# Four places of weight matrices in rotation: expert 0's first matrix loaded in the projection, the first half of the tokens routed earlier

## The reference

```
x = x + attn(layernorm(x)) @ Wr + br          # 2048 tokens, D = 1024, 16 heads of 64; mask multiplies the scores
f = layernorm(x)
p = softmax(f @ router_w + router_b)          # 8 experts, the best two of a token, weighted with their p
shared = gelu(f @ sw1 + sb1) @ sw2 + sb2      # hidden 2048
mixed  = sum over the two chosen experts of p_e * (gelu(f @ rw1[e] + rb1[e]) @ rw2[e] + rb2[e])
x = x + shared + mixed
```

## Time and profile before

| | us |
|---|---|
| median of 3 runs | 1258.63 (1258.38 to 1302.35) |
| the profiled execution | 1259.96 |
| its span, slowest core (core 2) | 1258.4 |
| spans of the 8 cores | 1252.9 to 1258.4 |
| PE busy | 1134.6 (90%) |
| ACT, DVE, POOL busy | 505.7, 446.3, 225.1 |
| HBM read, written | 241.40 MB, 74.45 MB |

### The profile page before, as it was taken

How to read it: one execution, slowest core, us unless ns; L and a number is a source line. 1 busy time by engine, 2 the same in 40 slices (tenths; PEclk the granted TensorE clock), 3 DMA queues, 4 the chain that set the end, 5 groups by cost and what they waited for, 6 DMA issues and landing times.

```text
span 1258.4 us, 20967 instructions; the slowest of 8 cores (1252.9 to 1258.4 us)
## 1 busy us (share of the span) xinstructions
PE 1134.6 (90%) x7570; PEld 595.2 (47%) x7648; DVE 446.3 (35%) x617; ACT 505.7 (40%) x671; POOL 225.1 (18%) x389
## 2 busy tenths in 40 slices
PE   5988888888889989519999999999999999999998
PEld 3533333333334434217475757565666666444443
DVE  6456667767657740000101010101111010134476
ACT  5768888888862233213131322222222221122100
POOL 1022222222210017501111111111111110212230
PEclk9999999999999979859999999999999999999999
DMA  6769557673756529999999999996969995485484
GB/s 191 258 182 226 135 135 117 175 162 106 115 118 231 199 80 238 241 203 188 189 200 252 244 200 192 192 272 111 255 128 199 190 192 114 149 288 194 150 302 167
DMA packets 66212, 235.34 MB, mean 187 GB/s; under 512 B 8256, under 2 KB 9152, under 8 KB 64576
## 3 DMA queue, kind: packets, MB, share of 16 engines
q0 software_dynamic: 34592, 123.87, 51.3%
q1 hardware_dynamic: 31520, 110.10, 25.8%
HBM read 241.40 MB, written 74.45 MB: 251 GB/s over the span
## 4 chain that ended last, share of the span: by engine, by line
PE 76%; DVE 7%; issue 7%; DMA 4%; ACT 4%; POOL 2%; DVEq 0%; another core or an unknown queue 0%; SPq 0%; ACTq 0%; POOLq 0%
PE PM L810 20%; PE PM L825 17%; PE PM L774 9%; PE PM L754 6%; PE SLOT L646 4%; PE PM L714 4%; PE NUM L664 4%; PE DEN L671 3%; ACT PT L1184 3%; DVE RC L931 3%; PE PM L832 2%; DMA XTILE<-xe 2%; POOL xe L517 2%; DMA xe<-XN,IDX 2%; DVE DS L922 2%
## 5 line engine op out<-in xcount | busy, mean ns | idle before, releaser
L1184 ACT ACTIVATE PT<-SLOT 128x1024 bf16<-128x1024 f32 (+1 forms) x320 | 262.6, 903 | 44.5 <-PE SLOT L646 43.7
L1108 DVE TENSOR_TENSOR YST<-PM,B2BC 128x512 f32<-128x512 f32 x64 | 44.2, 691 | 476.2 <-PE PM L825 442.5
L1240 ACT ACTIVATE HE_T<-PM,B1ALL 128x576 bf16<-128x576 f32 x128 | 94.9, 741 | 254.0 <-PE PM L810 254.0
L664 PE MATMUL NUM<-PT,VX 128*64 128x512 bf16 (+3 forms) x640 | 115.4, 360 | 18.6 <-DVE NS L919 15.1
L810 PE MATMUL PM<-XET,WB 128*128 128x288 bf16 x1024 | 127.8, 288 | 1.4 <-ACT XET L1223 1.1
L810 PE MATMUL PM<-XET,WA 128*128 128x288 bf16 x1024 | 126.1, 286 | 0.0
L646 PE MATMUL SLOT<-QT,KT 64*128 64x512 bf16 (+3 forms) x640 | 100.6, 354 | 17.7 <-ACT PT L1184 13.8
L671 PE MATMUL DEN<-PT,ONES 128*64 128x512 bf16 (+3 forms) x640 | 110.4, 349 | 5.9 <-DVE DS L922 5.9
L810 PEld LDWEIGHTS PM<-XET,WB 128*128 128x128 bf16 x1024 | 100.5, 98 | 28.8 <-issue 3.0
L825 PE MATMUL PM<-WB,HE_T 128*128 128x512 bf16 x496 | 113.0, 379 | 0.8
L825 PE MATMUL PM<-WA,HE_T 128*128 128x512 bf16 x497 | 112.2, 379 | 0.8
(11 more groups left out here) (124 smaller groups left out, 1129.1 us busy)
## 6 DMA issues: line engine op xcount, KB each, us to landing
WA<-w2cat POOLq DMA_DIRECT2D x48, 512.0 KB, 13.8
WA<-w1cat POOLq DMA_DIRECT2D x40, 512.0 KB, 24.1
WB<-w1cat POOLq DMA_DIRECT2D x40, 512.0 KB
XT<-xtok SPq DMA_DIRECT2D x32, 512.0 KB, 3.8
wbf<-WA SPq DMA_DIRECT2D x8, 2048.0 KB, 6.8
yd<-YST SPq DMA_DIRECT2D x32, 512.0 KB, 9.6
WB<-w2cat POOLq DMA_DIRECT2D x24, 512.0 KB, 23.3
xe<-ZERO SPq DMA_DIRECT2D x16, 512.0 KB, 5.1
```

What stands on the lines that cost most here:

```text
L664: e.matmul(NUM[64 * hh:64 * hh + 64, lo:512], VX[:, kc * D + c * 128 + 64 * hh:kc * D + c * 128 + 64 * hh + 64], pt(n)[:, hh * 512 + lo:(h ...
L1184: e.activation(heads(pt(n), lo, 512), heads(slot(r), lo, 512), AF.Exp, scale=0.125).then_inc(expd, 1)
L1240: e.activation(HE_T[:, ht * CAP:(ht + 1) * CAP].rearrange("p (h q) -> p h q", h=2), heads(PM1[:, (n % 2) * 1024:(n % 2 + 1) * 1024], 0, CA ...
```

## The change

Expert 0's first matrix goes to `WA2` (was V's place) and its second to `WB1`; even experts use `WA2` and `WB1`, odd ones `WA1` and `WB2`. The hidden halves that are spilled, and the x1 rows at the end, move to `WB2`; so ACT waits for the stores of x1 before it writes the second half. POOL issues the 8 pieces of expert 0's first matrix in the projection, one behind each of the first 8 tiles, and no longer between the scatters. The scatters of half 0 start at projection tile 14. `choose(0)` comes one tile sooner on DVE and `place(0)` two, `positions(0)` follows them on PE. Three small constants are loaded from ACT's queue instead of SP's.

```diff
--- before.py
+++ after.py
...
@@ -273,7 +274,7 @@
                 ZERO = sb(s1, "ZERO", [128, 2 * D], BF16)
             SB2BC = sb(s, "SB2BC", [128, D], F32)
 
-        G12, X1D = WA1.ap().bitcast(F32), WA2.ap().bitcast(F32)
+        G12, X1D = WA1.ap().bitcast(F32), WB2.ap().bitcast(F32)
 
         with ExitStack() as p:
             XTR = ps(p, "XTR", [128, 4 * 1024], BF16)
@@ -308,14 +309,14 @@
             return XLN2T[:, at:at + n]
 
         def w_first(x):
-            return WA1 if x % 2 else WB1
+            return WA1 if x % 2 else WA2
 
         def w_second(x):
-            return WA2 if x % 2 else WB2
+            return WB2 if x % 2 else WB1
 
         def hidden(k):
 
-            return (XLN2T[:, 0:8192], WA2[:, 8192:16384], H1D[:, 0:8192], H1D[:, 8192:16384])[k]
+            return (XLN2T[:, 0:8192], WB2[:, 8192:16384], H1D[:, 0:8192], H1D[:, 8192:16384])[k]
 
         def wbf_rows(x, i):
             return wbf[x * 256 + i * 128:x * 256 + (i + 1) * 128, :]
@@ -334,10 +335,6 @@
 
         def run_sync(e):
             for t in range(NMT):
-                if t == 1:
-                    e.dma_start(out=EPS[:], in_=c_eps).then_inc(eps_in, 16)
-                    e.dma_start(out=IDB[:], in_=c_idb).then_inc(idb_in, 16)
-                    e.dma_start(out=ONES[:], in_=c_ones).then_inc(ones_in, 16)
                 if t >= 4:
                     e.wait_ge(xb_done, t - 3)
                 e.dma_start(out=ring(XT, t % 4), in_=xtok[t * 128:(t + 1) * 128, :]).then_inc(xt_in[t % 4], 16)
@@ -468,7 +465,7 @@
 
         def spill(e, k):
             e.dma_start(out=h1d[k * 128:(k + 1) * 128, :],
-                        in_=WA2[:, k * 8192:(k + 1) * 8192]).then_inc(h1_out, 16)
+                        in_=WB2[:, k * 8192:(k + 1) * 8192]).then_inc(h1_out, 16)
 
 
         def run_gpsimd(e):
@@ -510,30 +507,34 @@
                         e.dma_start(out=BRR[:], in_=br_row).then_inc(brr_in, 16)
                         e.dma_start(out=RWW[:], in_=rww_rl).then_inc(rww_in, 16)
 
-            e.wait_ge(zero_out, 16 * 3 * NE)
+            e.wait_ge(av_mm, len(SCORES))
+            for i in range(PIECES):
+                e.wait_ge(op_mm, i + 1)
+                piece(WA2, w1cat[1], i, w1_in[0])
 
 
             def scatter(k, t):
                 e.indirect_dma_start(xe, bass.IndirectOffsetOnAxis(IDX[:, k * NMT + t:k * NMT + t + 1], 0),
                                      xn2(t), None).then_inc(scat, 16)
 
+            e.wait_ge(zero_out, 16 * 3 * NE)
             e.wait_ge(rt, RT_IDX)
-            e.wait_ge(op_mm, NMT)
             for t in range(HALF):
                 for k in range(2):
-                    e.wait_ge(s_mm1, 2 * t + k + 1)
+                    n = 2 * t + k
+                    if n < 6:
+                        e.wait_ge(op_mm, 14 + n // 2)
+                    else:
+                        e.wait_ge(s_mm1, n - 5)
                     scatter(k, t)
-                piece(WB1, w1cat[1], t, w1_in[0])
             e.wait_ge(rt, RT_HALF + RT_IDX)
             for t in range(HALF, NMT):
-                e.wait_ge(s_mm1, HALF + t + 1)
+                e.wait_ge(s_mm1, t + 3)
                 for k in range(2):
                     scatter(k, t)
 
-            e.wait_ge(xn2_done, NMT)
-            for j in range(4):
-                e.wait_ge(x1_out[j], 16 * 4)
-            load(WB2, w2cat[1], w2_in[0])
+            e.wait_ge(op_mm, NMT)
+            load(WB1, w2cat[1], w2_in[0])
 
 
             for x in range(1, NEXP):
@@ -700,8 +701,6 @@
                 m.then_inc(pos_mm, 1)
 
             for i in range(NMT + 3):
-                if i == HALF + 6:
-                    positions(0)
                 if i < NMT:
                     t = i
                     if t >= 2:
@@ -715,6 +714,8 @@
                                      WRF[:, kc * D + h * 512:kc * D + (h + 1) * 512], start=(kc == 0), stop=False)
                         m = e.matmul(psv, ONES[0:1, 0:128], BRR[0:1, h * 512:(h + 1) * 512], start=False, stop=True)
                     m.then_inc(op_mm, 1)
+                if i == HALF + 4:
+                    positions(0)
                 if 2 <= i < NMT + 2:
                     t = i - 2
                     e.wait_ge(xn2_done, t + 1)
@@ -726,12 +727,11 @@
                         m = e.transpose(TR[:, (t % 2) * 1024 + c * 128:(t % 2) * 1024 + (c + 1) * 128],
                                         xn2(t)[:, c * 128:(c + 1) * 128], IDB[:])
                     m.then_inc(tr_mm, 1)
-
-                for t in {HALF + 3: [], HALF + 4: [HALF, HALF + 1]}.get(i, [i - 3]):
-                    if t < 0:
-                        continue
+                if i >= 3:
+                    t = i - 3
                     e.wait_ge(tr_ev, t + 1)
                     if t == HALF:
+
                         e.wait_ge(rt, 1)
                     for c in range(NCH):
                         m = e.matmul(PM2[:, t * 8:(t + 1) * 8], xln2t(c, t), RWW[:, c * NE:(c + 1) * NE],
@@ -739,7 +739,7 @@
                     m.then_inc(lg_mm, 1)
 
             def shared_first(k):
-                W = WA1 if k < AHEAD else WB1
+                W = WA1 if k < AHEAD else WA2
                 for ht in range(16):
                     n = 16 * k + ht
                     if n == 0:
@@ -772,7 +772,7 @@
                     for kc in range(16):
                         at = kc * 512 + (i // 2) * 128
                         m = e.matmul(psv, hidden(k)[:, at:at + 128],
-                                     WB2[:, kc * D + (u % 2) * 512:kc * D + (u % 2 + 1) * 512],
+                                     WB1[:, kc * D + (u % 2) * 512:kc * D + (u % 2 + 1) * 512],
                                      start=(kc == 0), stop=(kc == 15))
                     m.then_inc(s_mm2, 1)
 
@@ -1065,9 +1065,9 @@
                 e.wait_ge(st2_done, 2 * t + 2)
                 e.bn_aggr(MV2[:, 2 * t:2 * t + 2], STAT2[:, t * 12:t * 12 + 12]).then_inc(mv2_done, 1)
 
-                if t == HALF + 3:
+                if t == HALF + 2:
                     choose(0)
-                elif t == HALF + 6:
+                elif t == HALF + 4:
                     place(0)
             normalise2(NMT - 1)
             choose(1)
@@ -1149,6 +1149,9 @@
 
 
         def run_scalar(e):
+            e.dma_start(out=EPS[:], in_=c_eps).then_inc(eps_in, 16)
+            e.dma_start(out=IDB[:], in_=c_idb).then_inc(idb_in, 16)
+            e.dma_start(out=ONES[:], in_=c_ones).then_inc(ones_in, 16)
             e.wait_ge(eps_in, 16)
 
             def evacuate(t):
@@ -1204,7 +1207,11 @@
             evacuate2(NMT - 1)
 
             def shared_gelu(k):
-                to = WA2[:, k * 8192:(k + 1) * 8192] if k < AHEAD else hidden(k)
+                to = WB2[:, k * 8192:(k + 1) * 8192] if k < AHEAD else hidden(k)
+                if k == 1:
+
+                    for j in range(4):
+                        e.wait_ge(x1_out[j], 16 * 4)
                 for ht in range(16):
                     n = 16 * k + ht
                     if k == 3 and ht == 0:
...
```

More of the change, by code:

```diff
@@ L421, in run_sync @@
                 e.dma_start(out=WA1[:], in_=wbf[bass.ds(x * 256, 128), :]).then_inc(ov_in, 16)
-                e.dma_start(out=WA2[:], in_=wbf[bass.ds(x * 256 + 128, 128), :]).then_inc(ov_in, 16)
+                e.dma_start(out=WB2[:], in_=wbf[bass.ds(x * 256 + 128, 128), :]).then_inc(ov_in, 16)
                 e.dma_start(out=B1X[:], in_=b1cat[bass.ds(x * 128 + 128, 128), :]).then_inc(ov_in, 16)
@@ L859, in run_tensor @@
                         m = e.matmul(PM2[:, h * 512:(h + 1) * 512], HE_T[:, kc * CAP:kc * CAP + 128],
-                                     WA2[:, kc * D + h * 512:kc * D + (h + 1) * 512], start=(kc == 0), stop=(kc == 15))
+                                     WB2[:, kc * D + h * 512:kc * D + (h + 1) * 512], start=(kc == 0), stop=(kc == 15))
                 m.then_inc(ov_m2, 1)
```

## The result

The changed kernel takes 1250.09 us in the median (20 runs) beside 1260.31 us for the kernel before on the same chip (20 runs). The ratio is 0.9925, with a 95% interval of 0.9911 to 0.9940. The medians are 10.2 us apart and the ratio stands for 9.4 us, where 18.6 us were forecast. In some executions of most kernels here the cores of one die show a lower granted clock and the time is some per cent longer; medians are over all executions, while ratios, and times given without a ratio, leave these out. The profiled execution took 1249.36 us, its slowest core (6) has a span of 1247.8 us, and the spans of the eight cores run from 1241.8 to 1247.8. Spans fell by 10.6 us, as the profiled time did.

The account below looks back on a forecast made before the run. A routing chain of indices, scatters and expert 0's rows was taken as the bound. Start -1.3, routing -1, projection +8 and first expert matmul at S + 80 gave 18.6 us less: 1240 us, range 1231 to 1251.

Parts of the forecast that it names:

- the late scatters: Rival, shared pass: scatters still end at S + 62 (S: start of shared pass), gain 8.6 us, 1250 us; chance 0.18.
- the last 64 rows: Rival, before expert 0: these rows load only at block 32, first matmul S + 90, gain 8 us, 1250; chance 0.07.
- Start, -1.3 us: Program start: without the constants ahead of it, SP's second x load goes out sooner, saving 1.3 us, bounds 0 and 1.4.
- Routing two tiles sooner, -1 us: Projection: routing work spread earlier shortens TensorE's waits for ACT, saving 1 us, bounds 0 and 2.
- Pieces in the projection, +8 us: Projection: eight tiles need 6.5 us of DMA each where TensorE takes 4.95, costing 8 us, between 3.5 and 12.4.
- A lead absorbs part: Projection: x loads issued 12.8 us ahead leave 8.9 us spare against the 12.4 us overload, counted between fully and nothing.
- "slower" rival: Projection: x starves, TensorE idles and its clock falls to 0.5; the gain is gone at 26.6 us lost; chance 0.05.
- Scatters home at S + 52: Shared pass: scatters finish at S + 52 in place of S + 76.4, bounds S + 44.5 and S + 62.
- the unexplained 13 us: Kernel before, first scatter to last landing: 72 us against 59 us of priced traffic; the remainder was read as unequal engines.
- Rows 21.7 us, first expert matmul at S + 80: Before expert 0: rows take 21.7 us from issue to first transpose, at S + 73.7; expert matmuls start 6.2 us later.
- From S on, a gain of 24.3 us: Shared pass start to first expert matmul: forecast S + 80, where the profiled kernel before had S + 104.3.
- ACT's new wait, the experts: Shared pass and experts: ACT's wait for x1 stores costs nothing, and expert matrices arrive in time, so nothing is given back.

Follow-up runs that it names:

- e10: The kernel before with only the three constants moved to ACT's queue; 1261.19 us, ratio 1.0003.
- e1: The changed kernel with expert 0's eight first-matrix pieces read from an already bf16 array, half the source bytes; 1236.31 us, ratio 0.9813.
- e2: The changed kernel with expert 0's first matrix issued behind the 32 scatters instead of in the projection; 1248.51 us, ratio 0.9903.
- e9: The changed kernel with pieces 1 to 4 behind tiles 1 to 4 and pieces 5 to 8 behind tiles 13 to 16; 1245.14 us, ratio 0.9881.
- e4: The changed kernel with a piece behind every second projection tile; 1238.97 us, ratio 0.9833.
- e6: The changed kernel with routing, scatter pacing and constants as before, keeping only the new places and moved pieces; 1258.43 us, ratio 0.9980.
- e3: The changed kernel with the pieces behind tiles 9 to 16 instead of 1 to 8; 1250.22 us, ratio 0.9886.
- e11: e4 with the spill and `SB2BC` behind the loads of expert 0's rows, and `B2BC` loaded ahead of the spill; 1243.03 and 1240.99 us, no ratio.
- e8: e4 with the spill and `SB2BC` behind the loads of expert 0's rows, and scatters not waiting for tile or block counts; 1257.03 us, ratio 0.9972.

## Where the prediction held and where it failed

The time lies in the stated range, but half of the forecast gain is missing. 1250 is also the number of two rivals, the late scatters and the last 64 rows, and neither of them happened: the number was met by another mechanism.

*Start, -1.3 us.* Wrong: 0. e10 gives 1.0003. I took a wait of 2.66 us in the second tile for one of the whole program; the second tile's statistics came sooner, the first tile's later, and the end stayed.

*Routing two tiles sooner, -1 us.* Right within its bounds of 0 and 2: the clean projection of e1 and e2 takes 88.2 us in place of 90.1.

*Pieces in the projection, +8 us.* This is the step that failed, and its failing part is the sentence "A lead absorbs part". The mechanism and the engine times were right: 3.0 us for x, and 3.6 us for a piece against 3.5. With 3.6 the overload is 8 x (6.6 - 4.95) = 13.2 us in place of 12.4. Against the clean projection the pieces cost 99.3 - 88.2 = 11.1 us in the median core, and 103.8 - 88.2 = 15.6 in the slowest. The lead of 8.9 us that I let count by half absorbed nothing of e9's first four pieces. I had the reason beside it, that a load waits for a store, and still took the middle. The landing of a store shows it. Stores of x1 in the changed kernel, core 6:

```profile
DMA to landing us min/median/max: 2.8/7.2/18.9
```

Before, core 2:

```profile
DMA to landing us min/median/max: 2.6/3.6/4.0
```

The lead was measured in quiet traffic. A load is issued 12.8 us ahead only while the store before it lands in 3.6 us; with stores of 7.8 to 18.9 us, one behind another in the chain, it isn't. It is these long ones that matter and not the median: in e4 (core 1) the stores land in 8.7 us in the median but in 11.9 at the most, and in e1, where the work fits, the loads of core 3 land in 6.4 us in place of 3.9 and nothing is lost. So a lead does cover landings that are somewhat longer; it did not cover a pile of work.

Once TensorE stands, its granted clock falls too, by the windows of core 6 (us, busy by engine from PE to POOL, granted clock, DMA share, GB/s):

```profile
385.00:395.00 10.00, 8.93 (x51) 3.51 (x48) 4.54 (x8) 1.41 (x3) 1.20 (x3) 1.00 1.03 206
395.00:405.00 10.00, 7.42 (x34) 2.73 (x34) 3.56 (x6) 1.41 (x3) 0.05 (x1) 0.66 1.02 224
405.00:415.00 10.00, 7.67 (x59) 3.65 (x59) 4.49 (x8) 2.82 (x6) 1.05 (x2) 1.00 0.85 203
```

The granted clock is 0.66 in one of them, a mix of its two levels (1.2 and 2.4 GHz), after TensorE had begun to stand; 34 matmuls are done in it where 51 and 59 are done beside it, in part because they wait. How much the clock costs is not separated, and it does not explain why core 6 is the slowest: core 2, whose projection takes 99.0 us, has the same granted clock of 0.93 over 371 to 470 us. That part stays open. TensorE idling for x at a lower clock is the mechanism of the "slower" rival, at half of its size: it would have needed 26.6 us. The 358 GB/s of the Trainium skill ("DMA: Bandwidth & Descriptors", Specifications) would have made the loss 0 to 7.4 us, by the prediction's estimate from that figure. The measured 11.1 lies outside that, and the price by the rows' engine time is nearer.

*Scatters home at S + 52.* Right: S + 51.5 in the slowest core, S + 52.6 in the median one. So the unexplained 13 us of the kernel before went with the pieces, as e6 shows by itself, and the rival of late scatters (S + 62) is out. Why pieces and scatters together took longer than the sum of the two stays open; the reading as unequal engines was not tested.

*Rows 21.7 us, first expert matmul at S + 80.* Right: 21.8 and 80.4. TensorE's wait for the rows was forecast at 13 us and is 14.9. The sign that the load of the rows would be issued 18 to 20 us sooner failed, with 11.1 us (526.44 against 537.49), because S itself came 13.9 us later. The last 64 rows made no wait of their own.

*From S on, a gain of 24.3 us.* Right for the profiled core, 25.3. But core 2 of the kernel before stood in one of the pauses on ACT and POOL. The median core had 102.0 us there, not 104.3, so that 21.6 us were to be had in it.

*ACT's new wait, the experts.* Right: TensorE waits for no matrix, and the stages behind kept their length.

Together for the slowest core: start 1.6 us worse than forecast, projection 6.6 us worse (13.6 against 7), S to the first expert matmul 1.0 better, behind it 0.9 worse. 18.6 - 1.6 - 6.6 + 1.0 - 0.9 = 10.5 us, up to rounding the 10.6 by which the profiled time fell.

## What to carry to other kernels

When a transfer is moved into a stage, add its engine time to that of the stage per tile and compare with the tile's period, and let no lead of a ring count against the excess if its loads wait for stores in the same traffic. Where pieces followed tile after tile, this sum gave 13.2 us (changed kernel), 7.2 (e3), 7.2 (e9) and 0 (e1), and the runs showed 11.1, 7.9, 8.2 and 0.0. The cure is spacing: the same eight pieces cost 11.1 us behind eight tiles running and 3.4 us behind every second one. And follow each transfer that is put behind another to the next one in its queue: e11 won 4.8 us in front of expert 0 and lost them at expert 1.

## What the runs showed of the hardware

- A piece that is cast from f32 takes the 16 engines 3.6 us for 0.52 MB written, one from a bf16 source 1.6 us; which fits a cost by the source's bytes.
- A store's landing grows from 3.6 to 7.2 us in the median, and to 18.9 at the most, while its own engine time stays at 1.5 us.
- ACT pauses for 3 to 12 us at a time, and POOL for up to 5, on one die, with no cause that the profile shows; without pacing of the scatters (e8) ACT's pauses add up to 24.3 us in one core. The DMA share is 1.01 in one of them (before, core 2) and 0.63 in another (e8, core 1). The cause stays open.
